# Weights summed over head groups ahead, a three-operation turn, joint normalisation of two softmaxes, and operands padded to 128 rows

## The chip, the cores and the metric

The kernel is one program on one NeuronCore of a Trainium2 chip. The metric is the device time of one execution in microseconds (us). TensorE is called PE here (its weight loads PEld), VectorE DVE, ScalarE ACT, GpSimd POOL, SyncE SP.

## The reference

Twelve layers of a decoder run one after the other over a residual of 16 batches x 128 positions x 256: four times an attention, a cross attention and a feed-forward part. The layers that the change touches are four attentions. Cut to what matters:

```
L1 attention (l1a):   q = rope(x Wq)  # 16 query heads of 16 in 4 groups
                      k = rope(x Wk), v = x Wv      # 4 heads of 16
                      # a group's queries act as one: only their sum over the group matters
                      out = softmax(causal(sum_g q . k) / 4) v Wo
L1 cross (l1x):       16 heads of 128 over 128 context rows, with a mask of context rows
L2 attention (l2a):   16 query heads, 4 key heads of 16, rms norm, rope, gain, causal softmax
L2 cross (l2x):       16 heads of 16, layer norm of q and k (affine w, b);
                      softmax over context rows 0..111 and another over rows 112..127,
                      each with its own value product; the two results are added
```

## The kernel before

Each layer is a block of its own with its own semaphores; a barrier stands between two layers, so what one layer saves the next cannot use in any other way than by starting earlier. The names of tiles begin with the layer: `l1a_`, `l1x_`, `l2a_`, `l2x_`.

**Small attentions** (`small_attention_layer`, line 3230: kind "summed" is l1a, "grouped" l2a, "split" l2x, "axial" l0x). All engines walk the same list of steps `STEPS`, and within a step each engine has a fixed order of parts; what is in flight are several batches at once. For batch b: DVE takes moments (`moments`), normalises (`normalise`), and splits into two float16 halves (`lower_norm`, line 3695); PE turns the result (`turn_norm`, line 3409), ACT copies it (`keep_norm`), PE projects (`project`, line 3421, six matmuls over halves and the two 128-row pieces of the width); DVE adds the bias (line 3720 or 3754, 3798 to 3806) and prepares q and k: for l1a in `summed_turned` (lines 3725 to 3743), which sums 256 query columns over groups to 64, copies 64 key columns, multiplies four times by cos or sin, and adds or subtracts four times. ACT and POOL then split q and k in halves (`upper_q`, `lower_q`, line 4140; `upper_k`, `lower_k`, line 4146).

Scores are made twice. `scores` (line 3494) has queries in rows; DVE reduces them to a maximum (`find_max`, line 3841), which `keep_max` (3848) writes as one more column, number KS = 48, behind the halves of q in tile `zq`. PE turns `zq` again (`turn_again`, 3507), ACT keeps it as `q2T`, and `scores_by_key` (3524 in l2a, 3535 elsewhere) computes scores with keys in rows and the maximum already subtracted: its operands have KX = 49 rows. In l2a the left operand is a slice of 49 rows of `kT`; `diagonal`, a tile into which SP's DMA spreads 48 rows of `kT` per row slot (line 3394), serves `scores` alone. ACT takes the exponential (3981), PE multiplies with the values (`heads_out`, 3553), DVE divides (`keep_out`, 3858 and 3864; in l2x twice for the two softmaxes, and 3870 adds them), ACT and POOL split the result (4037, 4151), PE turns and projects it (`turn_out` 3564, `project_out` 3572), and DVE adds it to the residual (3877).

In l1a a step is one batch, and `keep_busy` puts 11 matmuls of 256 columns without use (line 3441) into each step from that on which makes the scores of the second batch. In l2a and l2x a batch takes two steps.

**Context attention** (`context_attention_layer`, kind "merged" is l1x). Four chunks per batch, 64 in all. In each, PE adds the mask to the scores' bank by one matmul of one row (`one_row`, `mrow_b`, line 2763: 1 row x 128 columns against 1 row x 512), ahead of the 12 score matmuls (2771) and behind the 24 of the projection (2802). `mrow_b` is filled by DVE once a batch (line 2977).

## Time and profile before

| | |
|---|---|
| median of 3 runs | 3204.16 us (3202.68 to 3210.98) |
| the profiled execution | 3199.97 us |
| its span in the trace | 3198.2 us |
| PE, PEld, DVE, ACT, POOL busy | 88%, 67%, 71%, 59%, 54% |

| stage | from to, us | long, us | PE busy | DVE busy | ACT busy | POOL busy | clock granted |
|---|---|---|---|---|---|---|---|
| l1a | 588 to 737 | 149 | 120.0 | 98.2 | 68.7 | 37.1 | 0.83 |
| l1x | 737 to 1082 | 345 | 331.2 | 255.4 | 221.1 | 172.0 | 0.98 |
| l2a | 1283 to 1500 | 217 | 196.0 | 161.9 | 120.9 | 113.4 | 0.97 |
| l2x | 1500 to 1758 | 258 | 183.5 | 194.4 | 173.2 | 176.8 | 0.91 |

How to read it: an average over a stage does not tell what bounds it. The end time that the trace gives a matmul is modelled; the distance between the starts of two rows on PE is what the first one took of the engine. An engine in these stages can be busy 85% and still be the one that all others wait for, since the drains between its dependent operations are not counted as busy. The granted clock is the share of TensorE's full 2.4 GHz: 0.50 is the level of 1.2 GHz.

### The profile page before, as it was taken

Reading aid. Unit: us, or ns where it says so; the run is one execution under the profiler, and the core shown is the slowest. Engines: PE = TensorE matmul, PEld = TensorE weight load, DVE = VectorE, ACT = ScalarE, POOL = GpSimd, SP = SyncE. Lnnn points to the kernel's source line nnn. Section 1 sums busy time; section 2 is a strip of 40 time slices with the busy share of each in tenths; the row PEclk is TensorE's granted clock in tenths of the full one; section 3 lists DMA queues with packets and bytes.
Section 4 is the critical chain, followed back from the end, with each engine's and each line's share of the span. In section 5 each row is a group of like instructions: output and inputs, shape, how many; then the busy total and the mean of one; then the engine's idle time right before and its main releaser. Section 6 shows DMA issues by size and latency. Waiting matters only on the chain. (4 is left out here: it accounts for less than half of the span.)

```text
span 3198.2 us, 72026 instructions
## 1 busy us (share of the span) xinstructions
PE 2829.3 (88%) x25704; PEld 2153.0 (67%) x25739; DVE 2268.1 (71%) x5486; ACT 1887.5 (59%) x3629; POOL 1714.2 (54%) x1824
## 2 busy tenths in 40 slices
PE   7969989798999885797687899899999799998998
PEld 5757775456888654575466555688888677776665
DVE  5567764665777641786786777677777688888787
ACT  3346763355666422464676565566666588886675
POOL 2122211223555456563874366688888589887800
PEclk9999999799999886899899899999999999999999
DMA  4010001000000345000000632000000000001000
GB/s 164 1 23 14 14 9 67 7 2 8 10 7 5 121 112 117 10 6 24 13 16 14 252 89 73 3 1 0 0 0 0 6 8 6 5 5 41 29 1 27
DMA packets 95168, 104.64 MB, mean 33 GB/s; under 512 B 40716, under 2 KB 82125, under 8 KB 91984
## 3 DMA queue, kind: packets, MB, share of 16 engines
q1 hardware_dynamic: 90328, 96.08, 9.7%
q0 software_dynamic: 4608, 5.57, 1.1%
q8 instruction: 134, 2.20, 0.3%
q14 instruction: 98, 0.80, 0.1%
HBM read 80.84 MB, written 13.71 MB: 30 GB/s over the span
## 5 line engine op out<-in xcount | busy, mean ns | idle before, releaser
L2232 PE MATMUL bank<-l3a_ln_xnT,far 128*128 128x128 f16 x3072 | 194.4, 220 | 1.8 <-POOL l3a_ln_xnT L2046 1.8
L2232 PEld LDWEIGHTS bank<-l3a_ln_xnT,far 128*128 128x128 f16 x3072 | 181.7, 99 | 3.3 <-POOL l3a_ln_xnT L2046 2.2
L877 PE MATMUL bank<-l2f_xnT,l2f_wi 128*128 128x512 f16 x672 | 156.5, 381 | 7.0 <-POOLq L741 6.4
L3553 PE MATMUL bank<-l0x_v,l0x_pT 128*128 128x128 f32 x1024 | 133.9, 279 | 4.1 <-ACT l0x_pT L3981 2.5
L3553 PEld LDWEIGHTS bank<-l0x_v,l0x_pT 128*128 128x128 f32 x1024 | 126.8, 191 | 14.9 <-issue 5.8
L1226 PE MATMUL bank<-l3f_xnT,near 128*128 128x512 f16 x480 | 120.6, 388 | 6.9 <-DVE l3f_xnT L1011 3.5
L3146 POOL TENSOR_TENSOR l1x_prob<-l1x_prob,l1x_srec 128x512 f32<-128x512 f32 x64 | 66.7, 1043 | 111.1 <-DVE l1x_srec L2911 111.1
L1241 PE MATMUL bank<-near,l3f_h 128*128 128x256 f16 x960 | 119.1, 274 | 5.1 <-DVE l3f_h L1016 2.2
L877 PEld LDWEIGHTS bank<-l2f_xnT,l2f_wi 128*128 128x128 f16 x672 | 65.3, 98 | 77.8 <-POOLq L741 9.9
L1241 PEld LDWEIGHTS bank<-near,l3f_h 128*128 128x128 f16 x960 | 93.9, 98 | 34.4 <-DVE l3f_h L1016 4.1
L3841 DVE TENSOR_REDUCE l0x_smax<-bank 128x4 f32<-128x512 f32 x128 | 86.3, 686 | 29.1 <-PE bank L3494 27.0
L1025 DVE SCALAR_TENSOR_TENSOR x_res<-bank,l3f_combine,x_res 128x256 f32<-128x256 f32 x256 | 105.6, 476 | 0.1
L3981 ACT ACTIVATE l0x_pT<-bank 128x512 f32<-128x512 f32 x128 | 73.0, 596 | 52.6 <-PE bank L3535 52.6
L705 DVE TENSOR_TENSOR l2f_h<-l2f_h 128x512 f16<-128x512 f32 x56 | 59.8, 1069 | 57.6 <-ACT l2f_h L817 57.6
L2802 PE MATMUL bank<-l1x_ln_xnT,far 128*128 128x128 f16 x1536 | 96.3, 219 | 3.3 <-DVE far L2897 1.4
L2802 PE MATMUL bank<-l3x_ln_xnT,near 128*128 128x128 f16 x1536 | 96.3, 219 | 2.6 <-DVE near L2897 1.4
L3054 ACT ACTIVATE l3x_prob<-bank,l3x_less,l3x_q_rr 128x128 f32<-128x128 f32 x256 | 96.7, 461 | 1.8 <-DVE l3x_less L2934 1.3
L2154 PE MATMUL bank<-far,l3a_oT 128*128 128x256 f16 x768 | 94.3, 273 | 1.4 <-DVE l3a_oT L2339 1.4
L2825 PE MATMUL bank<-far,l1x_oT 128*128 128x256 f16 x768 | 94.3, 273 | 0.4 <-DVE x_res L2968 0.3
L2825 PE MATMUL bank<-near,l3x_oT 128*128 128x256 f16 x768 | 94.3, 273 | 0.1
L3172 POOL TENSOR_TENSOR l1x_qT<-l1x_q,l1x_qT 128x512 f16<-128x512 f32 x64 | 74.1, 1158 | 37.0 <-ACT l1x_qT L3088 36.8
L2802 PEld LDWEIGHTS bank<-l3x_ln_xnT,near 128*128 128x128 f16 x1536 | 91.1, 98 | 4.0 <-DVE near L2897 1.8
(740 smaller groups left out, 9402.0 us busy)
## 6 DMA issues: line engine op xcount, KB each, us to landing
far<-in_l1f_in SPq DMA_DIRECT2D x32, 256.0 KB, 4.4
l2f_front<-l2f_shares SPq DMA_DIRECT2D x5, 1024.0 KB
sums<-near SPq DMA_DIRECT2D x2, 2176.0 KB, 19.3
far<-in_l1f_down SPq DMA_DIRECT2D x32, 128.0 KB, 5.0
far<-sums SPq DMA_DIRECT2D x8, 512.0 KB, 7.3
l2f_wi<-in_l2f_in SPq DMA_DIRECT2D x14, 256.0 KB, 5.9
far<-l0x_kT SPq DMA_DIRECT2D x64, 48.0 KB
far<-l2x_kT SPq DMA_DIRECT2D x32, 96.0 KB
```

Of the source, the lines that this page charges most:

```text
L877: last = nc.tensor.matmul(bank[:, :], wi16[n % 2][p][:, a, k, :], xnT[q][:, k, 512 * g:512 * g + 512], start=(k + p + q == 0), stop=(k == ...
L1025: last = nc.vector.scalar_tensor_tensor(core.x[:, b, :], bank_y(k, t), weight, core.x[:, b, :], ALU.mult, ALU.add)
L1226: last = nc.tensor.matmul(b_h[f % 2][:, :], wi16[p][:, n, k, :], xnT[q][:, k, 512 * g:512 * g + 512], start=(k + p + q == 0), stop=(k == K ...
L1241: last = nc.tensor.matmul(bank_y(k, t), h16[f % LAG][q][:, P * t:P * t + P], wd16[p][:, n, :], start=(begins and p + q == 0 and t % 2 == 0 ...
L2154: last = nc.tensor.matmul(b_y[:, 0:D], oT[c % 2][q][:, P * j:P * j + P], wo(HC * c + j, 0, D, p), start=(c + j + p + q == 0), stop=(c == N ...
L2232: last = nc.tensor.matmul(bank[:, P * j:P * j + P], w(k, 512 * c + P * j, P, p), norm.xnT[u][q][:, k, :], start=(k + p + q == 0), stop=(k ...
L2802: last = nc.tensor.matmul(b_q[:, P * j:P * j + P], wq(k, 512 * c_ + P * j, P, p), norm.xnT[u][q][:, k, :], start=(k + p + q == 0), stop=(k ...
L2825: last = nc.tensor.matmul(b_y[:, 0:D], oT[c_ % 2][q][:, P * j:P * j + P], wo(HC * c_ + j, 0, D, p), start=(c_ + j + p + q == 0), stop=(c_ ...
L3054: last = nc.scalar.activation(prob[c_ % 2][:, at], b_s[:, at], ACT.Exp, bias=less[c_ % 2][:, j:j + 1], scale=q_rr[c_ % 2][:, j:j + 1])
L3172: nc.gpsimd.tensor_tensor(qT[c_ % 2][1][:, :], q32[:, :], qT[c_ % 2][0][:, :], ALU.subtract).then_inc(q_lo, 1)
L3553: last = nc.tensor.matmul(b_o[:, at:at + P], pT[f % 3][:, j, :], v_all[b % NV][:, hv:hv + P], start=True, stop=True)
L3841: last = nc.vector.tensor_reduce(smax[g % 2][:, a, 4 * u:4 * u + 4], s[:, :, lo:hi], AX.X, ALU.max)
```

## The change

- **l1a.** At the layer's start DVE sums the query weights over each group of heads (`sum_groups`, 256 columns to 64, for both 128-row pieces) into a tile of 192 columns with the key and value columns beside them, and the bias in the same way. The projection, its bias addition and its buffers have 192 columns in place of 384. The turn becomes two multiplications of 128x128, even columns by (cos, sin) and odd columns by (-sin, cos), and one addition of 128x128 that writes q and k into one tile `tok`. One semaphore, `q_ready`, tells of both.
- **l2x.** The affine bias is added to q and k in one operation of 512 columns in place of two of 256. `keep_out` takes one reciprocal of 16 columns and one multiplication of 256 in place of two of 8 and two of 128.
- **l2a.** `scores_by_key` takes its left operand from `diagonal`, all 128 rows, against all 128 rows of `q2T`. For this the DMA spreads 49 rows in place of 48 and waits for `st_made` in place of `s_made`; and POOL clears column 48 of `zq` (a memset of 128x16) in each `lower_q`, since `scores` would otherwise read a maximum left from an earlier batch.
- **l1x.** `one_row` and `mrow_b` have 128 rows, of which 127 are zero; three memsets at the layer's start are added.

```diff
-            one_row = sb("one_row", [1, P], BF16)
-            mrow_b = [sb(f"mrow_b{u}", [1, HC, P], BF16) for u in range(2)]
+            one_row = sb("one_row", [P, P], BF16)
+            mrow_b = [sb(f"mrow_b{u}", [P, HC, P], BF16) for u in range(2)]
...
-                    nc.vector.memset(one_row[:, :], 1.0)
+                    nc.vector.memset(one_row[:, :], 0.0)
+                    for u in range(2):
+                        nc.vector.memset(mrow_b[u][:, :, :], 0.0)
+                    dve.drain()
+                    nc.vector.memset(one_row[0:1, :], 1.0)
...
-    QW = 384 if causal else D
+    QW = {"summed": 192, "grouped": 384}.get(kind, D)
...
-                        after(sp, s_made, UB * R * (b - 1))
+                        after(sp, st_made if kind == "grouped" else s_made, UB * R * (b - 1))
                         for r in range(UB):
-                            rows = slice(SLOT * r, SLOT * r + KS)
+                            rows = slice(SLOT * r, SLOT * r + (KX if kind == "grouped" else KS))
...
                     if kind == "grouped":
-                        rows = slice(SLOT * u, SLOT * u + KX)
-                        last = nc.tensor.matmul(bank[:, :], kT[b % NK][rows, g % R, :],
-                                                q2T[g % 2][rows, :, :].rearrange("p j q -> p (j q)"),
+                        last = nc.tensor.matmul(bank[:, :], diagonal[b % 2][:, g % R, u, :],
+                                                q2T[g % 2][:, :, :].rearrange("p j q -> p (j q)"),
                                                 start=False, stop=True)
...
+                    if kind == "summed":
+                        for k in range(KD):
+                            sum_groups(wide_w["q"][:, k, :], weights["q"][:, k, :])
...
+                def sum_groups(to, w):
+                    nc.vector.tensor_reduce(to[:, 0:64].rearrange("p (h d) -> p h d", h=4),
+                                            w[:, 0:D].rearrange("p (h g d) -> p h d g", h=4, g=4), AX.X, ALU.add)
+                    nc.vector.tensor_copy(to[:, 64:], w[:, D:])
...
-                    nc.vector.tensor_reduce(pair[:, 0, :, :], raws[b % 2][:, 0:D].rearrange("p (h g d) -> p h d g", h=4, g=4),
-                                            AX.X, ALU.add)
-                    nc.vector.tensor_copy(pair[:, 1, :, :], raws[b % 2][:, D:D + 64].rearrange("p (h d) -> p h d", h=4))
...
+                    for a, n in enumerate(("cos", "sin")):
+                        turn = consts[n][:, :].rearrange("p (c d) -> p c d", c=2).unsqueeze(1).to_broadcast([P, 8, 2, 8])
+                        nc.vector.tensor_tensor(parts_[a], x[:, :, a, :].unsqueeze(2).to_broadcast([P, 8, 2, 8]), turn,
+                                                ALU.mult)
...
+                    nc.vector.tensor_tensor(tok[b % 2][:, :, :].rearrange("p h d -> p (h d)"), rot[:, 0:P], rot[:, P:2 * P],
+                                            ALU.add).then_inc(q_ready, 1)
...
-                        nc.vector.tensor_tensor(tok[:, :, :], four(raws[b % 2][:, :])[:, i, :, :], sb_[:, i, :, :], ALU.add
-                                                ).then_inc(ready, 1)
+                    nc.vector.tensor_tensor(tok[b % 2][:, :, :].rearrange("p (a h) d -> p a h d", a=2),
+                                            four(raws[b % 2][:, :]), sb_, ALU.add).then_inc(q_ready, 1)
...
-                    for a in range(parts):
-                        nc.vector.reciprocal(orec[:, a, 0:n], o[:, :, (HD + 1) * (a + 1) - 1])
+                    nc.vector.reciprocal(orec[:, 0:n, :], o[:, :, :, HD])
...
+                        nc.vector.tensor_tensor(o_two[:, 0:n, :, :], o[:, :, :, 0:HD],
+                                                orec[:, 0:n, :].unsqueeze(3).to_broadcast([P, n, parts, HD]), ALU.mult
+                                                ).then_inc(o_read, 1)
...
+                    if kind == "grouped":
+                        nc.gpsimd.memset(z[:, :, KS:KX], 0.0)
```

DVE in l1a, from the bias addition of one batch (`l1a_raw`) to the next residual, before:

```order
L3720 SCALAR_TENSOR_TENSOR l1a_raw<-bank,l1a_t_bias 128x384
L3681 BN_STATS l1a_stats<-x_res 128x6
L3683 BN_AGGR l1a_mv<-l1a_stats 128x2
L3685 TENSOR_SCALAR l1a_var<-l1a_mv 128x1
L3848 TENSOR_SCALAR l1a_zq<-l1a_smax 128x4
L3725 TENSOR_REDUCE l1a_pair<-l1a_raw 128x64
L3727 COPY l1a_pair<-l1a_raw 128x64
L3733 TENSOR_TENSOR l1a_rot<-l1a_pair,l1a_t_cos 128x64
L3734 TENSOR_TENSOR l1a_rot<-l1a_pair,l1a_t_sin 128x64
L3735 TENSOR_TENSOR l1a_rot<-l1a_pair,l1a_t_sin 128x64
L3736 TENSOR_TENSOR l1a_rot<-l1a_pair,l1a_t_cos 128x64
L3742 TENSOR_TENSOR l1a_q_tok<-l1a_rot 128x4x8
```

and now:

```order
L3735 SCALAR_TENSOR_TENSOR l1a_raw<-bank,l1a_bias 128x192
L3696 BN_STATS l1a_stats<-x_res 128x6
L3698 BN_AGGR l1a_mv<-l1a_stats 128x2
L3700 TENSOR_SCALAR l1a_var<-l1a_mv 128x1
L3853 TENSOR_SCALAR l1a_zq<-l1a_smax 128x4
L3744 TENSOR_TENSOR l1a_rot<-l1a_raw,l1a_t_cos 128x128
L3744 TENSOR_TENSOR l1a_rot<-l1a_raw,l1a_t_sin 128x128
L3749 TENSOR_TENSOR l1a_tok<-l1a_rot 128x128
L3883 SCALAR_TENSOR_TENSOR x_res<-bank,x_res 128x256
```

The reduction and the copy are gone, ten operations of the turn (with the three more additions that follow the last row above) have become three.

POOL in l2a, where a batch's q is split (`l2a_zq`), before:

```order
L4111 TENSOR_TENSOR l2a_rstd<-l2a_var,minus_half 128x1
L4140 TENSOR_TENSOR l2a_zq<-l2a_q_tok,l2a_zq 128x16x16
L4151 TENSOR_TENSOR l2a_o<-l2a_o_tok,l2a_o 128x256
L4116 TENSOR_TENSOR x_res<-x_res,l2a_t_out_bias 128x256
L4146 TENSOR_TENSOR l2a_zk<-l2a_k_tok,l2a_zk 128x4x16
```

and now:

```order
L4117 TENSOR_TENSOR l2a_rstd<-l2a_var,minus_half 128x1
L4147 MEMSET l2a_zq 128x16
L4148 TENSOR_TENSOR l2a_zq<-l2a_tok,l2a_zq 128x16x16
L4159 TENSOR_TENSOR l2a_o<-l2a_o_tok,l2a_o 128x256
L4122 TENSOR_TENSOR x_res<-x_res,l2a_t_out_bias 128x256
```

One memset stands ahead of the split of q; nothing else has moved there. On PE no matmul changes its place in any of the four layers: operands and widths alone differ.

DVE in l2x, from the second reciprocals of a batch to the maximum behind q and k, before:

```order
L3858 RECIPROCAL l2x_orec<-bank 128x8 x2
L3864 TENSOR_TENSOR l2x_o_two<-bank,l2x_orec 128x128 x2
L3870 TENSOR_TENSOR l2x_o_tok<-l2x_o_two 128x128
L3826 TENSOR_TENSOR l2x_raw<-l2x_raw,l2x_rr 128x512
L3831 TENSOR_TENSOR l2x_q_tok<-l2x_raw,l2x_t_affine_b 128x256
L3831 TENSOR_TENSOR l2x_k_tok<-l2x_raw,l2x_t_affine_b 128x256
L3841 TENSOR_REDUCE l2x_smax<-bank 128x4 x2
```

and now:

```order
L3862 RECIPROCAL l2x_orec<-bank 128x16
L3868 TENSOR_TENSOR l2x_o_two<-bank,l2x_orec 128x256
L3872 TENSOR_TENSOR l2x_o_tok<-l2x_o_two 128x128
L3832 TENSOR_TENSOR l2x_raw<-l2x_raw,l2x_rr 128x512
L3836 TENSOR_TENSOR l2x_tok<-l2x_raw,l2x_t_affine_b 128x512
L3846 TENSOR_REDUCE l2x_smax<-bank 128x4 x2
```

Three pairs have become one operation each; the order is the same.

## Rows read from the trace of the kernel before

**Rows 1.** Stretch, length, busy PE, PEld, DVE, ACT, POOL; clock, DMA share, GB/s.
```profile
600.00:620.00 20.00, 13.22 (x56) 6.03 (x57) 16.60 (x62) 6.17 (x18) 6.42 (x13) 0.50 0.00 2
850.00:900.00 50.00, 50.00 (x580) 41.13 (x578) 38.81 (x79) 33.86 (x66) 28.20 (x33) 1.00 0.03 8
```

**Rows 2.** Timeline of PE in l1a at full clock: start us, us, idle before.
```profile
655.32 1.15 PE L3421 MATMUL bank<-l1a_w_q,l1a_xnT 128*128 128x384 f16 x6
...
661.12 0.27 PE L3564 MATMUL bank<-ident,l1a_o 128*64 128x128 f16 x2 [0.26 <-ACT l1a_xnT L3947]
...
662.75 1.15 PE L3421 MATMUL bank<-l1a_w_q,l1a_xnT 128*128 128x384 f16 x6
```

**Rows 3.** The same in l1a's first steps.
```profile
596.85 0.61 PE L3409 MATMUL bank<-ident,l1a_xn 128*128 128x128 f16 x4 [0.19 <-DVE l1a_xn L3695]
600.02 2.08 PE L3421 MATMUL bank<-l1a_w_q,l1a_xnT 128*128 128x384 f16 x6 [2.57 <-DVE l1a_raw L3720]
603.92 0.61 PE L3409 MATMUL bank<-ident,l1a_xn 128*128 128x128 f16 x4 [1.82 <-DVE l1a_xn L3695]
...
629.89 0.61 PE L3409 MATMUL bank<-ident,l1a_xn 128*128 128x128 f16 x4
```

**Rows 4.** Timeline of DVE in l1a's first steps.
```profile
598.61 0.80 DVE L3690 TENSOR_SCALAR l1a_xn<-x_res,l1a_mv,l1a_rstd 128x256 f32<-128x256 f32 x1 [1.82 <-POOL l1a_rstd L4111]
...
600.79 0.58 DVE L3725 TENSOR_REDUCE l1a_pair<-l1a_raw 128x64 f32<-128x256 f32 x1
...
603.44 0.43 DVE L3695 TENSOR_TENSOR l1a_xn<-l1a_xn 128x256 f16<-128x256 f32 x1
```

**Rows 5.** Timeline of PE in l1x.
```profile
901.53 1.50 PE L2802 MATMUL bank<-l1x_ln_xnT,far 128*128 128x128 f16 x24
902.87 0.39 PE L2025 MATMUL bank<-ident,l1x_ln_xn 128*128 128x128 f32 x2
...
906.58 1.50 PE L2802 MATMUL bank<-l1x_ln_xnT,far 128*128 128x128 f16 x24
908.01 0.38 PE L2763 MATMUL bank<-l1x_mrow_b,l1x_one_row 1*128 1x512 bf16 x1
908.33 0.84 PE L2771 MATMUL bank<-l1x_cT,l1x_qT 128*128 128x128 f16 x12
```

**Rows 6.** Timeline of PE in l2a's last steps.
```profile
1448.69 0.38 PE L3484 MATMUL bank<-l2a_mask_b,l2a_ident_b 128*128 128x512 bf16 x1
1448.90 0.82 PE L3494 MATMUL bank<-far,l2a_qT 128*128 128x256 f16 x4
1449.56 0.38 PE L3520 MATMUL bank<-l2a_maskT_b,l2a_ident_b 128*128 128x512 bf16 x1
1449.87 0.39 PE L3524 MATMUL bank<-l2a_q2T,l2a_kT 49*128 49x512 f16 x1
1450.19 0.39 PE L3520 MATMUL bank<-l2a_maskT_b,l2a_ident_b 128*128 128x512 bf16 x1
```

**Rows 7.** Timeline of DVE in l2a, steady.
```profile
1384.63 0.26 DVE L3858 RECIPROCAL l2a_orec<-bank 128x16 f32<-128x16 f32 x1 [0.63 <-PE bank L3553]
...
1393.37 0.41 DVE L3695 TENSOR_TENSOR l2a_xn<-l2a_xn 128x256 f16<-128x256 f32 x1
```

**Rows 8.** Timeline of PE in l2a, steady.
```profile
1382.36 0.40 PE L3409 MATMUL bank<-ident,l2a_xn 128*128 128x128 f16 x4 [0.15 <-DVE l2a_xn L3695]
```

**Rows 9.** Line 3770 by itself: durations as min/median/max in ns, starts.
```profile
L3770 DVE TENSOR_TENSOR l2a_rot<-l2a_raw,l2a_t_sin x32: 312/795/847, 1294.6 to 1460.0; 128x160 f32<-128x160 f32 x32
```

**Rows 10.** Timeline of POOL in l2a, steady.
```profile
1390.13 0.88 POOL L4151 TENSOR_TENSOR l2a_o<-l2a_o_tok,l2a_o 128x256 f16<-128x256 f32 x1 [4.54 <-ACT l2a_o L4037]
```

**Rows 11.** Timeline of POOL in l2x, steady.
```profile
1625.87 5.45 POOL L4134 TENSOR_TENSOR l2x_rr<-l2x_ss,minus_half 128x32 f32<-128x32 f32 x1
```

**Rows 12.** Timeline of DVE in l2x, steady.
```profile
1631.35 0.69 DVE L3826 TENSOR_TENSOR l2x_raw<-l2x_raw,l2x_rr 128x512 f32<-128x512 f32 x1
1632.18 0.44 DVE L3831 TENSOR_TENSOR l2x_q_tok<-l2x_raw,l2x_t_affine_b 128x256 f32<-128x256 f32 x1
```

More of the change, by code:

```diff
@@ L3342, in small_attention_layer @@
             whole, angles_ready = sb("whole", [P, NB, HD], I32), sem("angles_ready")
-        q_tok = [sb(f"q_tok{u}", [P, H, HD]) for u in range(2)]
-        k_tok = [sb(f"k_tok{u}", [P, HK, HD]) for u in range(2)]
+        tok = [sb(f"tok{u}", [P, H + HK, HD]) for u in range(2)]
+        q_tok, k_tok = [t[:, 0:H, :] for t in tok], [t[:, H:, :] for t in tok]
         if kind == "summed":
-            rot, pair = sb("rot", [P, D]), sb("pair", [P, 2, 4, 16])
+            rot = sb("rot", [P, D])
         if kind == "grouped":
@@ L3351, in small_attention_layer @@
         if kind != "axial":
-            raws = [sb(f"raw{u}", [P, 512 if split else 384]) for u in range(2)]
+            raws = [sb(f"raw{u}", [P, 512 if split else QW]) for u in range(2)]
         if kind in ("grouped", "split"):
@@ L3700, in axial @@
                                                    (q_made, q_read, q_ready, zq_ready))
[L3701 removed]
+                    src, to = (b_kv[:, 0:D], k_tok[b % 2]) if second else (b_q[:, 0:D], q_tok[b % 2])
                     dve.wait_ge(made, b + 1)
@@ L3712, in axial @@
                     dve.drain()
-                    nc.vector.tensor_tensor(tok[:, :, :], tok[:, :, :], r, ALU.add).then_inc(ready, 1)
+                    nc.vector.tensor_tensor(to[:, :, :], to[:, :, :], r, ALU.add).then_inc(ready, 1)
                 def summed(b, stage):
@@ L3739, in summed_turned @@
                     after(dve, zq_ready, b - 1)
-                    for i, (tok, ready) in enumerate(((q_tok[b % 2], q_ready), (k_tok[b % 2], k_ready))):
-                        s = slice(4 * i, 4 * i + 4)
-                        nc.vector.tensor_tensor(tok[:, :, 0:8], turns_[0][:, s, :], turns_[1][:, s, :], ALU.subtract)
-                        nc.vector.tensor_tensor(tok[:, :, 8:16], turns_[2][:, s, :], turns_[3][:, s, :], ALU.add)
-                        dve.drain().then_inc(ready, 1)
+                    nc.vector.tensor_tensor(tok[b % 2][:, :, :].rearrange("p h d -> p (h d)"), rot[:, 0:P], rot[:, P:2 * P],
+                                            ALU.add).then_inc(q_ready, 1)
                 def grouped(b, stage):
@@ L3862, in keep_out @@
                     out = o_tok[:, first:first + n, :]
-                    for a in range(parts):
-                        last = nc.vector.tensor_tensor(o_two[:, a, 0:n, :] if split else out,
-                                                       o[:, :, (HD + 1) * a:(HD + 1) * a + HD],
-                                                       orec[:, a, 0:n].unsqueeze(2).to_broadcast([P, n, HD]), ALU.mult)
-                    last.then_inc(o_read, 1)
                     if split:
+                        nc.vector.tensor_tensor(o_two[:, 0:n, :, :], o[:, :, :, 0:HD],
+                                                orec[:, 0:n, :].unsqueeze(3).to_broadcast([P, n, parts, HD]), ALU.mult
+                                                ).then_inc(o_read, 1)
                         dve.drain()
-                        nc.vector.tensor_tensor(out, o_two[:, 0, 0:n, :], o_two[:, 1, 0:n, :], ALU.add)
+                        nc.vector.tensor_tensor(out, o_two[:, 0:n, 0, :], o_two[:, 0:n, 1, :], ALU.add)
+                    else:
+                        nc.vector.tensor_tensor(out, o[:, :, 0, 0:HD],
+                                                orec[:, 0:n, 0].unsqueeze(2).to_broadcast([P, n, HD]), ALU.mult
+                                                ).then_inc(o_read, 1)
                     if first + n == H:
```

36 lines of the change are left out of this document (16 added, 20 removed).

## Prediction

> **What bounds the kernel now.** I read the stage table first, then the busy time by stretches, then in each touched layer the timeline of PE, and of DVE and POOL where PE waits for them. Busy shares mislead here: l1a and l2a show PE at 81% and 90% of the stage, and only the waits printed on its rows tell which engine sets the pace.
>
> - l1a at the full clock: PE. The projection (L3421) starts at 655.32 and 662.75, a step of 7.43 us, and what PE waits for in between is ACT, a quarter of a us before `turn_out` [rows 2]. DVE is named by no wait there.
> - l1a in its first steps: the clock is 0.50 and PE is busy 13.2 of 20 us, DVE 16.6 [rows 1]. PE waits 1.82 us for DVE's `lower_norm` [rows 3]. In front of that operation DVE turns a batch, from the reduction at 600.79 to 603.44, 2.65 us [rows 4].
> - l1x: PE alone, 50.00 of 50.00 us at clock 1.00 [rows 1].
> - l2a: PE and DVE close the step together. DVE waits 0.63 us for `heads_out`, then works from 1384.63 to `lower_norm`'s end at 1393.78, 9.15 us in which no row shows a wait [rows 7], and PE waits 0.15 for a `lower_norm` before it turns the next batch [rows 8]. PE's own work beside those 9.15 us has slack.
> - l2x: the loop goes through DVE (`keep_out`, then affine, then the maximum), ACT, POOL and back to PE.
>
> **l1a.** Of the turn, the reduction, a copy, four products and four sums become two products and a sum. The chain of 2.65 us [rows 4] becomes three operations of 128 columns with a drain between the second and third; a 256-column operation costs 0.43 there [rows 4], so I take about 1.1 us for all, plus 0.2 off the narrower bias addition: 1.75 us less. The projection streams 6 x 192 = 1152 columns less, 0.96 us at 1.2 GHz and 0.48 at 2.4.
>
> First steps: from the turn at 596.85 to that at 629.89 lie five intervals, 33.04 us [rows 3]. In the first two the wait for DVE closes the loop, and each can give up to 1.75; the wait of 1.82 in the first covers it, that of the second is 1.05, and its PE part shrinks too. The other three have no wait in front of `turn_norm`: they give the projection's 0.96, a little more where ACT and DVE are also in the loop; I take 1.2, 1.0 and 1.5. Sum 7.2. The next interval, in which the clock rises, gives 0.8.
>
> Full clock: nine further steps, bound by PE [rows 2], 9 x 0.48 = 4.3. The sums of weights at the start add three reductions and three copies on DVE, up to 3 x (0.58 + 0.43) = 3.0 by rows 4, less what narrower casts save; DVE stands idle 1.82 there for POOL's `rstd` [rows 4], and the first projection waits for later things, so I take 0 and keep +1.2 (3.0 - 1.8) as the end. l1a: 7.2 + 0.8 + 4.3 = **-12.3**, from -16 (each of the first five intervals gives 1.75) to -9 (the three middle ones 0.5 each, the start +1.2).
>
> **l1x.** The trace has one-row matmuls between 128-row ones. 24 projections take 902.87 - 901.53 = 1.34 us when a 128-row operation follows, and 908.01 - 906.58 = 1.43 when the one-row mask does: 0.09 to go in. The mask takes 908.33 - 908.01 = 0.32 [rows 5]; a full-height matmul of 512 columns takes 1448.90 - 1448.69 = 0.21 [rows 6]: 0.10 to come out, beyond rounding. With all rows padded both should go, 0.19 a chunk. 62 of the 64 chunks lie in stretches like 850 to 900 where PE never idles: 62 x 0.19 = 11.8. That the gap belongs to the change of height, not to this mask, l2a supports: its 49-row matmul costs the same on both sides, 0.31 and 0.32 against 0.21 [rows 6]. Three memsets at the start, two of 512 columns, stand ahead of DVE's first copy for PE: three times 0.2, +0.7 with the drain. l1x: **-11.1**, from +0.7 (no gap closes) to -13.
>
> The Trainium skill, page "TensorEngine Tiling (Array Packing)", section "Key Properties", says that changing the tiling mode drains TensorE. The 0.10 us on either side in rows 5 and 6 agree with it.
>
> **l2a.** Two 49-row matmuls per step, with two gaps of 0.10 each, would give 0.41 a step, twice a batch; if PE alone set the pace, 32 x 0.41 = 13.1. But in the steady steps the loop closes through DVE's 9.15 us [rows 7, 8]: PE finishes its scores sooner and waits more for `lower_norm`. So nothing there. In the last eight steps, which follow rows 6, no batch is normalised or prepared any more and the chain is PE, ACT, PE: four of them give 0.41, four 0.15, since ACT's exponential stands between. 2.3 us.
>
> Against this: line 3770 on DVE takes 0.31 at its shortest and 0.80 at its median [rows 9], while POOL runs an operation with two inputs. A shift of POOL's row 4151 against DVE moves such delays about. In 1390.13's step POOL splits the output for 0.88 us after 4.54 us of idleness [rows 10]; it starts when ACT has copied what PE's shorter step releases about 0.4 earlier, and then covers another DVE operation. I take +0.1 a batch over some 13 batches, +1.3, from -0.2 to +0.5 (the 0.49 between minimum and median, once a batch): -3 to +6.5. POOL's memset of 16 columns falls into the idle 4.54; its cover gone it would cost some 0.1 to 0.2 a batch. SP's DMA now waits for `st_made`, which PE passes before it turns the next k, so nobody behind it on SP's queue waits more. The 49th row adds a fiftieth to each DMA. l2a: **-1**, from -6 to +5.
>
> **l2x.** DVE's affine pair takes 0.44 each, 0.88; one operation of 512 columns is like L3826, 0.69 [rows 12]. That is 0.2, and with the start of the second one saved I estimate 0.3 (0.2 to 0.4) less on the way to the maximum, 14 steady batches: -4. The joint division takes off DVE some 0.4, but L3826 starts at 1631.35, just as POOL's `rr` ends (1625.87 + 5.45 = 1631.32) [rows 11, 12]: DVE reaches it earlier and waits. Nothing. l2x: **-4**, from 0 (another wait closes the loop instead) to -6 (14 x 0.4).
>
> Sum: -12.3 - 11.1 - 1 - 4 = -28.4. The profiled execution took 3199.97, so its counterpart is 3171.6. The median of the three runs before lies 4.2 above the profiled one, the fastest 2.7; I add 2.7 and say **3174 us**. All four terms at their ends would give 3202.7 - 41 = 3162 (-16 - 13 - 6 - 6) and 3202.7 - 3.3 = 3199 (-9 + 0.7 + 5 + 0); they won't all fall on one side.
>
> **Rivals.**
>
> *The padding gives nothing.* The gap at a one-row matmul could belong to its operands (a new bank, bfloat16 beside float16) and stay: L3484 is bfloat16 ahead of float16 and shows 0.21 [rows 6], which speaks against it. l1x then +0.7, l2a's tail 0: -12.3 + 0.7 + 1.3 - 4 = -14.3, 3188. The Trainium skill, page "TensorE: Matmul & The Clock Gate", section "Step-by-step: what each phase is for", says that the row count doesn't matter for a weight load; by that rule alone padding buys nothing. Rows 5 and 6 show a difference beside 1 and 49 rows, which the rule doesn't cover.
>
> *POOL and DVE take l2a's and l2x's gains back.* The shift costs 0.5 a batch, +7.5 in 15 batches of l2a, and l2x's merged operation falls beside a POOL operation and gains nothing: -12.3 - 11.1 + 5.2 + 0 = -18.2, 3184. For it: the spread of rows 9; against: the shift has no reason to fall on the bad side every time. The Trainium skill, page "SBUF — State Buffer", section "🔬 SBUF: two separate sides", calls the port pair of the two an exclusive lock, which the first to start gets. The 0.31 against 0.80 of rows 9 agrees.
>
> *PE sets l2a's pace after all.* The waits of 0.63 and 0.15 [rows 7, 8] would then be slack on both sides, and 13.1 come off in place of 1: 3162. The unbroken 9.15 us speak against it.
>
> *Slower: the clock stays low in l1a.* While the clock stands at 0.50, PE is busy two thirds of the time [rows 1], and it rose only after steps in which it waited no more. With a third to a half less projection in each step PE could sit at 1.2 GHz to the layer's end. The projection takes 2.08 us at one level and 1.15 at the other [rows 2, 3], 1.8 times; a step of 7.43, all PE, would take up to 6 more at that ratio, and since part of it is not columns I take 4. Thirteen such steps: +53 on -28, so 3225; it decides from about seven steps on. Against it: `keep_busy` stays in each step, the waits for DVE shrink with the work, and what is left fills PE as before.
>
> **How the numbers follow.** The forecast has 0.64 (3164 to 3183 in itself), no gain from padding 0.12, the give-back on POOL 0.13, PE in l2a 0.07, the clock 0.04. To hold 8 in 10 the range takes in the forecast with its ends, the 3188 and the 3184, and most of the 3162: **3160 to 3190**. A measurement of this kernel tells 0.3% from no change, 9.6 us: faster means under 3194.5. Only the clock, and the bad ends of several terms at once, lie above: faster 0.93, same 0.04, slower 0.03.
>
> **What the profile after would show.** l1a: `turn_norm` in the first steps some 5.3 us apart in place of 7.07 (603.92 - 596.85), at the full clock the projection every 6.95 us. l1x: the mask matmul followed after 0.21 us and the stage 11 us shorter, PE still without idle time. l2a: 0.21 at the second matmul of `scores_by_key`, a longer wait of PE for `lower_norm`, about 1 us in place of 0.15, and the same step. l2x: `rr` waited for by DVE, the step some 0.3 shorter per batch. Wrong it would be by a clock of 0.50 in l1a past 640 us, by 0.3 at the padded mask, or by a median of the line that was 3770 that has moved.

## The result, and the profile after

| | before | after |
|---|---|---|
| median | 3207.48 us (3202.68 to 3210.98, 4 runs) | 3180.65 us (3178.75 to 3184.30, 4 runs) |
| ratio | | 0.9919 (95% interval 0.9900 to 0.9937) |
| span of the profiled execution | 3198.2 us | 3178.5 us |

The changed kernel is faster by 26 us, with 32 and 20 as the ends of the interval. The forecast was 3174, the range 3160 to 3190. The change itself was put at -28.4 us, inside those ends. The 3174 stands on the fastest run of the kernel before, 3202.68, and the median beside the changed kernel is 3207.48. Between the two profiled executions lie 19.7 us. Where they went, by the first operation of each layer on DVE (us):

| stage | before | after | difference | forecast |
|---|---|---|---|---|
| l1a | 151.11 | 140.95 | -10.2 | -12.3 |
| l1x | 342.59 | 333.83 | -8.8 | -11.1 |
| l2a | 217.15 | 214.80 | -2.3 | -1 |
| l2x | 258.43 | 256.01 | -2.4 | -4 |
| the four | | | -23.7 | -28.4 |
| all others | | | +4.0 | 0 |

The +4.0 are the cross attention of layer 0 with its feed-forward part (+2.7), the feed-forward part of layer 2 (+2.5) and that of layer 1 (-1.1). The feed-forward parts do the same work as before, and the kernels below show how far such stages wander: the cross attention of layer 0 took 303.1 to 308.6 us, the feed-forward part of layer 1 194.1 to 202.4, that of layer 2 265.0 to 268.2. The four changed stages wander too. In the profiles that left their code as it was, l1a took 148.1 to 151.2 us, l1x 341.6 to 344.8, l2a 216.5 to 218.8 and l2x 258.2 to 261.7. So a single profile tells a stage no better than to some us, which for l2a and l2x is as much as their difference in the table. That is why the readings below go by the distance of rows inside a layer.

**l1a.** PE's turns at 1.2 GHz, then two projections at the full clock (timeline of PE after: start, us, line, operation; idle before it in brackets), to set against [rows 2, 3]:

```profile
596.74 0.61 PE L3415 MATMUL bank<-ident,l1a_xn 128*128 128x128 f16 x4 [7.57 <-DVE l1a_xn L3710]
...
601.07 0.61 PE L3415 MATMUL bank<-ident,l1a_xn 128*128 128x128 f16 x4 [1.84 <-DVE l1a_xn L3710]
...
605.90 0.61 PE L3415 MATMUL bank<-ident,l1a_xn 128*128 128x128 f16 x4 [1.42 <-DVE l1a_xn L3710]
...
658.16 0.67 PE L3427 MATMUL bank<-l1a_w_q,l1a_xnT 128*128 128x192 f16 x6
...
665.12 0.67 PE L3427 MATMUL bank<-l1a_w_q,l1a_xnT 128*128 128x192 f16 x6
```

DVE's turn of a batch, to set against [rows 4]:

```profile
604.13 0.32 DVE L3744 TENSOR_TENSOR l1a_rot<-l1a_raw,l1a_t_cos 128x128 f32<-128x128 f32 x1
604.38 0.28 DVE L3744 TENSOR_TENSOR l1a_rot<-l1a_raw,l1a_t_sin 128x128 f32<-128x128 f32 x1
604.73 0.78 DVE L3749 TENSOR_TENSOR l1a_tok<-l1a_rot 128x128 f32<-128x128 f32 x1
605.43 0.41 DVE L3710 TENSOR_TENSOR l1a_xn<-l1a_xn 128x256 f16<-128x256 f32 x1
```

From 604.13 to `lower_norm` at 605.43 it is 1.30 us where it was 2.65. The addition took 0.78 in this batch, where POOL's bias addition (604.64 to 605.36) ran beside it; the median of the 16 is 0.31. The projection streams in 0.67 and starts every 6.96 us, where it was 7.43.

**l1x.** PE after, to set against [rows 5]:

```profile
895.93 1.50 PE L2802 MATMUL bank<-l1x_ln_xnT,far 128*128 128x128 f16 x24
897.27 0.38 PE L2763 MATMUL bank<-l1x_mrow_b,l1x_one_row 128*128 128x512 bf16 x1
897.48 0.83 PE L2771 MATMUL bank<-l1x_cT,l1x_qT 128*128 128x128 f16 x12
898.15 0.81 PE L2814 MATMUL bank<-l1x_pT,l1x_c 128*128 128x512 f16 x3
```

The mask is entered 1.34 us after the projection's start and left after 0.21. Both gaps are gone. But in one chunk of four PE now waits:

```profile
895.49 0.60 PE L2740 MATMUL bank<-ident,l1x_prob 128*128 128x128 f32 x4
895.93 1.50 PE L2802 MATMUL bank<-l1x_ln_xnT,far 128*128 128x128 f16 x24
```

```profile
900.11 0.60 PE L2740 MATMUL bank<-ident,l1x_prob 128*128 128x128 f32 x4
900.77 1.51 PE L2802 MATMUL bank<-l1x_ln_xnT,far 128*128 128x128 f16 x24
```

```profile
898.84 1.16 POOL L3176 TENSOR_TENSOR l1x_qT<-l1x_q,l1x_qT 128x512 f16<-128x512 f32 x1 [0.48 <-ACT l1x_qT L3092]
899.95 0.69 POOL L2046 TENSOR_TENSOR l1x_ln_xnT<-l1x_ln_whole,l1x_ln_xnT 128x256 f16<-128x256 f32 x1
```

The turn of the probabilities (L2740) is followed by the projection after 0.44 us in the first pair, after 0.66 in the second. What the second one needed is POOL's split of the batch's normalised input (L2046), which ended at 900.64; it stood behind the split of q (L3176).

The kernel before had this already in it. POOL and PE there:

```profile
910.60 0.68 POOL L2046 TENSOR_TENSOR l1x_ln_xnT<-l1x_ln_whole,l1x_ln_xnT 128x256 f16<-128x256 f32 x1
```

```profile
911.41 1.51 PE L2802 MATMUL bank<-l1x_ln_xnT,far 128*128 128x128 f16 x24
```

The split ended at 911.28, 0.13 us ahead of the projection. That is the same 0.13 as in the changed kernel (900.64 and 900.77), where PE did wait for it. PE was never idle, and POOL had nothing to spare.

**l2a.** PE, the second matmul of `scores_by_key` and the next turn; DVE, the ends of its chain, to set against [rows 6 to 8]:

```profile
1431.59 0.38 PE L3529 MATMUL bank<-l2a_q2T,far 128*128 128x512 f16 x1
1431.80 0.38 PE L3526 MATMUL bank<-l2a_maskT_b,l2a_ident_b 128*128 128x512 bf16 x1
1432.02 0.38 PE L3529 MATMUL bank<-l2a_q2T,far 128*128 128x512 f16 x1
1432.23 0.28 PE L3463 MATMUL bank<-ident,l2a_zk 128*128 128x128 f16 x2
1433.47 0.40 PE L3415 MATMUL bank<-ident,l2a_xn 128*128 128x128 f16 x4 [0.96 <-DVE l2a_xn L3710]
```

```profile
1378.06 0.26 DVE L3862 RECIPROCAL l2a_orec<-bank 128x16 f32<-128x16 f32 x1 [0.63 <-PE bank L3558]
...
1386.85 0.41 DVE L3710 TENSOR_TENSOR l2a_xn<-l2a_xn 128x256 f16<-128x256 f32 x1
```

0.21 in place of 0.32 after the matmul, and a wait of 0.96 in place of 0.15 for `lower_norm`. DVE's chain is 9.20 us long (1378.06 to 1387.26) where it was 9.15, and the step went from 11.48 to 11.54.

**l2x.** DVE and POOL, to set against [rows 11, 12]:

```profile
1611.53 0.69 DVE L3832 TENSOR_TENSOR l2x_raw<-l2x_raw,l2x_rr 128x512 f32<-128x512 f32 x1 [0.35 <-POOL l2x_rr L4140]
1612.36 0.70 DVE L3836 TENSOR_TENSOR l2x_tok<-l2x_raw,l2x_t_affine_b 128x512 f32<-128x512 f32 x1
1612.99 0.74 DVE L3846 TENSOR_REDUCE l2x_smax<-bank 128x4 f32<-128x448 f32 x2
```

```profile
1605.92 5.57 POOL L4140 TENSOR_TENSOR l2x_rr<-l2x_ss,minus_half 128x32 f32<-128x32 f32 x1
```

And DVE before, the maximum behind the pair of affine additions, the first of which starts at 1632.18 in [rows 12]:

```profile
1633.10 0.74 DVE L3841 TENSOR_REDUCE l2x_smax<-bank 128x4 f32<-128x448 f32 x2
```

The affine addition takes 0.63 from start to start where the pair took 0.92. DVE waits 0.35 for `rr`, as said; but `rr` itself takes 5.57 where it took 5.45.

### The profile page after: what moved, and what is told of

It is laid out like the page before. It is cut to its first block and busy times, and to the rows that moved or that the text cites. A ratio compares the mean times of both kernels' runs of the same rounds, so it can differ in the third digit from the quotient of the medians.

```text
span 3178.5 us, 71847 instructions
## 1 busy us (share of the span) xinstructions
PE 2810.5 (88%) x25739; PEld 2163.4 (68%) x25739; DVE 2230.1 (70%) x5303; ACT 1882.8 (59%) x3629; POOL 1717.0 (54%) x1840
## 3 DMA queue, kind: packets, MB, share of 16 engines
q0 software_dynamic: 4608, 5.57, 1.1%
## 5 line engine op out<-in xcount | busy, mean ns | idle before, releaser
L2802 PEld LDWEIGHTS bank<-l1x_ln_xnT,far 128*128 128x128 f16 x1536 | 89.7, 98 | 8.7 <-issue 3.5
L3176 POOL TENSOR_TENSOR l1x_qT<-l1x_q,l1x_qT 128x512 f16<-128x512 f32 x64 | 74.2, 1159 | 39.3 <-ACT l1x_qT L3092 39.2
```

What stands on the lines that cost most here:

```text
L2802: last = nc.tensor.matmul(b_q[:, P * j:P * j + P], wq(k, 512 * c_ + P * j, P, p), norm.xnT[u][q][:, k, :], start=(k + p + q == 0), stop=(k ...
L3176: nc.gpsimd.tensor_tensor(qT[c_ % 2][1][:, :], q32[:, :], qT[c_ % 2][0][:, :], ALU.subtract).then_inc(q_lo, 1)
```

## The experiments

Each kernel ran beside the kernel before on the same chip; differences in us are the ratio's distance from 1 times 3203.

**The l1a part alone** (the sums of weights, the narrow projection and the three-operation turn of the diff ahead).

> The kernel before with the l1a part of the change alone. My account: l1a shrinks from 151.1 us to about 141 (7 us of it in the five intervals between turns at 1.2 GHz, 3.3 in the seven intervals of steady steps, against a start that is 0.5 to 1.2 later), and nothing else moves: the profiled execution near 3190, a ratio near 0.9968. Rival, that the change's gains depend on each other: l1a gives clearly less or more than 10 us by itself. Rival, that the common tile for q and k costs something in the cross attention of layer 0 (its stage was 2.4 us longer in the profile after): that stage is 2 us longer here too, since this kernel has that tile as well.

Ratio 0.9976 (0.9965 to 0.9988), -7.7 us by the ratio. The stage took 139.75 us, and the intervals between turns were those of the changed kernel to 0.01 us, but for the one in which the clock rises (7.89 against 8.39). So the l1a gain stands by itself: the stage is 11.4 us shorter, and the interval of the ratio (3.8 to 11.2 us) holds the 10 expected, though its middle is lower. The cross attention of layer 0 took 307.2 us here; it took 308.4 in a kernel without the common tile for q and k and 304.4 in one with it, so the tile isn't its cause.

**The l1x part alone.**

> The kernel before with the l1x part alone: mask and ones padded to 128 rows, three memsets. My account: each chunk gives up the two gaps of 0.10 us beside the one-row matmul, 64 x 0.2 = 12.8; 3.0 of it come back because PE then reaches the projection of each new batch 0.22 us before POOL has split its normalised input, in 14 batches; +1.0 at the start. Stage from 342.6 to about 333.8, total near -8.8, a ratio near 0.9973. Rival, that the row count plays no role and the l1x gain came from elsewhere: no change here, L2763 still followed after 0.32.

Ratio 0.9969 (0.9959 to 0.9980), -9.9 us. The stage took 335.05, the mask 0.22 and 1.34, and the same wait in one chunk of four was there. The first mask came 0.4 us later after the layer's start than in the kernel before, not the 1.0 of the changed kernel.

**The l2a part alone.**

> The kernel before with the l2a part alone: scores by key with 128 rows. My account: PE's four matmuls per batch are 0.2 us faster each, PE waits 0.96 us for DVE before each turn in place of 0.15, and the steady step stays 11.5 us; the stage goes from 217.15 to about 214.8, by its first and last steps alone. Ratio near 0.9993. Rival, PE sets the pace: about 13 us less.

Ratio 0.9988 (0.9977 to 0.9998), -3.8 us with 0.6 and 7.4 as ends. The step was 11.54, the stage 215.97. As forecast: no gain in the steady step.

**The two halves of l2x, each alone.** First the affine addition:

```
-                    for i, (tok, ready) in enumerate(((q_tok[b % 2], q_ready), (k_tok[b % 2], k_ready))):
-                        nc.vector.tensor_tensor(tok[:, :, :], four(raws[b % 2][:, :])[:, i, :, :], sb_[:, i, :, :], ALU.add
-                                                ).then_inc(ready, 1)
+                    nc.vector.tensor_tensor(tok[b % 2][:, :, :].rearrange("p (a h) d -> p a h d", a=2),
+                                            four(raws[b % 2][:, :]), sb_, ALU.add).then_inc(q_ready, 1)
```

> The kernel before with the affine additions of l2x as one operation, the division of the two softmaxes as before. My account: DVE saves 0.29 us a batch on the loop; POOL's reciprocal square root of a batch (rr) is on the loop too and was 5.57 us after in place of 5.45. If that lengthening comes from the shorter keep_out (other operations of DVE beside it), it is absent here, and the step is 13.19 - 0.29 = 12.90; if it comes from the affine part's shift, it is here, and the step is 13.02. Stage about -4 or -2.4.

Ratio 0.9986 (0.9976 to 0.9996), -4.5 us. Steps of 12.90 to 12.91 but for one of 13.24, `rr` 5.44 to 5.45: the first of the two cases. The stage took 255.42, -3.0. Then the joint division alone (`keep_out` of the diff ahead):

> The kernel before with the two divisions of the softmaxes in l2x as one, the affine additions as before. My account: the division ends earlier and DVE then waits 0.35 us for POOL's rr; the step stays at 13.19 or gets 0.12 longer if the earlier operations of DVE fall beside rr and lengthen it. Stage 0 to +2 us. Rival, that the division is on the loop: 0.4 us a batch, -6.

Ratio 1.0005 (0.9995 to 1.0016), so the total doesn't tell this kernel from the one before. The step became 13.31 to 13.32, longer by 0.12, with `rr` at 5.57, but for one batch with `rr` at 5.44 and a step of 13.18. The stage took 261.27, which says nothing: it took 261.1 to 261.7 in three kernels with l2x as before. The batch with the short `rr` and the one behind it show what goes with what. DVE and POOL, first the batch with the short `rr`:

```profile
1615.13 5.44 POOL L4135 TENSOR_TENSOR l2x_rr<-l2x_ss,minus_half 128x32 f32<-128x32 f32 x1
```

```profile
1614.58 0.42 DVE L3863 TENSOR_TENSOR l2x_o_two<-bank,l2x_orec 128x256 f32<-128x256 f32 x1
1615.47 0.29 DVE L3867 TENSOR_TENSOR l2x_o_tok<-l2x_o_two 128x128 f32<-128x128 f32 x1 [0.46 <-issue]
```

and the next:

```profile
1628.31 5.57 POOL L4135 TENSOR_TENSOR l2x_rr<-l2x_ss,minus_half 128x32 f32<-128x32 f32 x1
```

```profile
1627.77 0.42 DVE L3863 TENSOR_TENSOR l2x_o_two<-bank,l2x_orec 128x256 f32<-128x256 f32 x1
1628.28 0.29 DVE L3867 TENSOR_TENSOR l2x_o_tok<-l2x_o_two 128x128 f32<-128x128 f32 x1
```

In the kernel before, DVE and POOL at the same place:

```profile
1639.12 0.34 DVE L3870 TENSOR_TENSOR l2x_o_tok<-l2x_o_two 128x128 f32<-128x128 f32 x1
```

```profile
1639.06 5.44 POOL L4134 TENSOR_TENSOR l2x_rr<-l2x_ss,minus_half 128x32 f32<-128x32 f32 x1
```

The addition of the two softmaxes (L3867, before L3870) reads two tiles in SBUF. Where it starts 0.03 us ahead of `rr`, `rr` is 0.13 longer: so in 9 batches here and in 9 of the changed kernel. Where it starts behind `rr`, `rr` is short: at +0.06 in 10 batches of the kernel before, with the addition at 0.34 in place of 0.29, and at +0.34 in the one batch here. The joint division brought the addition forward by about 0.1, onto the wrong side. The Trainium skill, page "SBUF — State Buffer", section "🔬 SBUF: two separate sides", says that a DVE operation with two inputs in SBUF and a GpSimd operation that reads SBUF exclude each other, the first to start keeping the port for the whole instruction. That the order of the two starts decides who pays agrees with it. The "whole instruction" does not: the addition ran inside the 5.44 us of `rr`, in those 10 batches too.

**POOL's order in l1x**, in the changed kernel:

```
                             norm.rsqrt(pool, b)
+                        if ln and c_ == 2:
+                            norm.second_half(pool, b, u)
                         if proj:
                             split_q(proj)
...
-                    if merged and ln and c_ == 2:
-                        norm.second_half(pool, b, u)
```

> The changed kernel with one thing moved: in l1x POOL splits the normalised input of a batch (line 2046) ahead of the split of q and not behind it. My account: PE's wait of 0.22 us before the projection of each new batch goes away, 14 x 0.22 = 3 us, and the chunks are 4.62 apart but for the one with the extra transposes. The split of q is 0.2 later, which has 1.5 us of slack. Total about 3 us below the changed kernel. Rival, that the 0.22 is no wait for POOL but something on PE: no change.

The stage went from 333.83 to 330.18; the distances of the masks are 4.62, 4.62, 4.62, 4.85 in place of 4.62, 4.85, 4.62, 4.85. From the first mask to the last it is 288.8 us, after 292.7 and before 302.4. POOL's split now ends 1.56 us ahead of the projection in place of 0.13. So the wait was POOL's. The median was 3178.37, the ratio 0.9915 (0.9898 to 0.9931), which by itself can't be told from the changed kernel's 0.9919; the stage can.

**384 columns again in l1a**, in the changed kernel:

```
-                            last = nc.tensor.matmul(b_q[:, 0:QW], xnT16[:, i, k, :], w16["q"][j][:, k, :],
+                            to, w = b_q[:, 0:QW], w16["q"][j][:, k, :]
+                            if kind == "summed":
+                                to = b_q[:, 0:384].rearrange("p (a n) -> p a n", a=2)
+                                w = w.unsqueeze(1).to_broadcast([P, 2, QW])
+                            last = nc.tensor.matmul(to, xnT16[:, i, k, :], w,
```

> The changed kernel with the projection of l1a streaming 384 columns again (the 192 twice), all else as changed. It tells the columns from the shorter turn on DVE. My account: the steady step of l1a goes back from 6.96 to 7.44 (+3.3 in seven intervals), the intervals at 1.2 GHz grow by up to 0.96 each where PE closes the loop (three of five) and by less where DVE does; about +8 in all, so that the turn on DVE alone is worth about 2 to 3 of the 10 us. Rival, DVE was the bound in the first steps: those keep their gain of 7, and only +4 come back.

The steady step went back to 7.44, as said, but the stage only to 143.13, +2.2 in place of +8. There are two reasons. The first is that the columns cost little in the first steps. The four intervals behind the second turn, all at 1.2 GHz, were 4.83, 3.89, 5.25 and 6.21 us; the changed kernel has 4.83, 3.80, 5.10 and 5.25, the kernel before 7.08, 5.12, 5.66 and 6.22. So the columns are worth 0, 0.09, 0.15 and 0.96 there, and only the fourth shows the projection's whole 0.96. In the first of them they only fill PE's wait for DVE, which is 0.46 in front of the third turn in place of 1.42. What the change gained in the first three intervals came nearly all from the shorter work on DVE: the expectation's rival was right for them.

The second reason is the clock. In the changed kernel and in this one (stretch, length, busy PE, PEld, DVE, ACT, POOL, then the granted clock, DMA share and GB/s):

```profile
621.31:626.31 5.00, 5.00 (x28) 2.74 (x26) 3.47 (x11) 3.73 (x8) 2.16 (x5) 0.50 0.00 2
631.31:636.31 5.00, 4.79 (x40) 2.98 (x39) 3.16 (x11) 2.44 (x5) 0.55 (x1) 0.87 0.00 0
```

```profile
616.57:621.57 5.00, 4.23 (x20) 2.09 (x21) 2.50 (x7) 1.38 (x5) 0.86 (x2) 0.50 0.00 0
621.57:626.57 5.00, 4.83 (x30) 2.40 (x29) 2.98 (x11) 3.95 (x9) 2.09 (x4) 0.66 0.01 3
626.57:631.57 5.00, 4.79 (x40) 3.12 (x39) 2.88 (x11) 3.33 (x9) 1.99 (x4) 1.00 0.01 3
```

Here it rose 33 us behind the layer's start, there 41, and the seven intervals from the second turn on sum to 39.2 us in place of 40.2, with the wider projection. Whether the columns did that is open. The moment wanders by itself: with l1a's code of before it came after 46 to 47 us in seven profiles and after 38 to 39 in two, both of them 148.1 us long as a stage in place of 151.0 to 151.2. Between the ratios of this kernel (0.9941, 0.9925 to 0.9958) and the changed one lie 7 us, with intervals that overlap.

**Two products left out of l2a's turn on DVE.** The multiplications by the sine (L3770) are left out in both kernels of this pair, so the output is another one; the first is otherwise the kernel before, the second has the padded scores by key.

```
-                    for i in range(2):
-                        lo, hi = 8 * i, 8 * i + 8
-                        nc.vector.tensor_tensor(r[:, :, lo:hi], x[:, :, 8 - lo:16 - lo],
-                                                consts["sin"][:, lo:hi].unsqueeze(1).to_broadcast([P, 20, 8]),
-                                                ALU.mult)
```

> The kernel before without the two multiplications by the sine in l2a's turn on DVE (that part of the computation is left out): 1.27 us less on DVE a batch. If DVE and PE both close the loop of l2a, PE with 0.15 us of slack, the step falls only by about 0.15 to 0.3, from 11.48 to some 11.2 to 11.35, and PE becomes the bound: -2 to -5 us. It is one half of a pair with the next kernel.

> As the last one (two multiplications by the sine left out of l2a's turn), with the 128-row scores by key added. The cut alone took the step of l2a from 11.48 to 11.16 and the stage from 217.15 to 212.3. My account, that PE sets the pace once DVE's chain is 1.27 us shorter: the padding then pays what it gives PE, 4 x 0.2 us a batch, until DVE is the bound again: a step of 10.4 to 10.7, and the stage 6 to 10 us below that of the cut alone, where the same padding was worth 1 to 2 us in the full kernel. Rival, the padding's gain doesn't reach PE's loop at all: the step stays at 11.16.

| | rows by key 49 | 128 | worth of the padding |
|---|---|---|---|
| DVE's turn whole: step, stage | 11.48, 217.15 | 11.54, 214.80 | +0.06, -2.3 |
| without the two products | 11.16, 212.27 | 10.80, 205.39 | -0.36, -6.9 |

```profile
1432.36 0.40 PE L3409 MATMUL bank<-ident,l2a_xn 128*128 128x128 f16 x4 [0.22 <-DVE l2a_xn L3694]
...
1443.15 0.40 PE L3409 MATMUL bank<-ident,l2a_xn 128*128 128x128 f16 x4 [0.22 <-DVE l2a_xn L3694]
```

The step lay a little above the 10.4 to 10.7 expected, for DVE is already the last again: PE waits 0.22 for its `lower_norm`, where it was 0.15 in [rows 8]. Where l2a was left as before, its stage took 216.5 to 218.8 us in seven profiles, and 214.1 to 216.0 in the five with the padding alone, so the -2.3 is known to about 1; the -6.9, with 0.36 a step in it, is of another size. Ratios 0.9994 (0.9984 to 1.0003) and 0.9972 (0.9960 to 0.9985).

**How many rows the mask needs.** The l1x part alone, with `one_row` and `mrow_b` of 64 and of 96 rows.

> The kernel before with the mask and the ones of l1x padded to 64 rows in place of 1. If the gap of 0.10 us on either side of a matmul is the price of another height of the array's tile (32, 64 or all 128 rows), 64 rows still pay it: the mask matmul is followed after 0.32 and entered after 1.43. If it is the price of a single row only, it is gone: 0.22 and 1.34.

> The same with 96 rows. By the account of tile heights 96 rows run as 128 and pay nothing: 0.22 and 1.34. If any operand with fewer than 128 rows pays, 0.32 and 1.43 as with 64 or 1.

```profile
900.23 1.50 PE L2802 MATMUL bank<-l1x_ln_xnT,far 128*128 128x128 f16 x24
901.67 0.39 PE L2763 MATMUL bank<-l1x_mrow_b,l1x_one_row 64*128 64x512 bf16 x1
901.99 0.84 PE L2771 MATMUL bank<-l1x_cT,l1x_qT 128*128 128x128 f16 x12
```

```profile
905.07 1.50 PE L2802 MATMUL bank<-l1x_ln_xnT,far 128*128 128x128 f16 x24
906.41 0.38 PE L2763 MATMUL bank<-l1x_mrow_b,l1x_one_row 96*128 96x512 bf16 x1
906.63 0.83 PE L2771 MATMUL bank<-l1x_cT,l1x_qT 128*128 128x128 f16 x12
```

64 rows pay 1.44 and 0.32, just as one row does; 96 rows take 1.34 and 0.22, just as 128 do. The steps say the same: 4.83 us from mask to mask in most chunks with 64 rows, 4.62 in every second one with 96. The stages took 344.23 and 335.27, the single execution of each kernel 3202.30 and 3192.24, against 3198.53 to 3206.90 in nine of the kernel before. That the gap belongs to the height of the tile into which the array is divided fits this, if 96 rows run at the full height; no trace shows which height an operand gets. The Trainium skill, page "TensorEngine Tiling (Array Packing)", section "Key Properties", says that a change of the tiling mode drains TensorE. A gap on both sides of the low matmul agrees with it.

**What the runs point to, together**: the changed kernel with POOL's order in l1x, with two divisions in l2x as before, and with the wide projection for the first six batches of l1a alone.

> The changed kernel with three edits that the runs so far point to. The divisions of l2x are two again: the step of l2x 12.90 in place of 13.02, POOL's rr 5.45, -1.5 us. POOL's order in l1x as in the run before: -3.6 in that stage. In l1a the first six projections stream the 192 columns twice, which holds PE busy while its clock is at 1.2 GHz: with 384 columns throughout the clock rose about 7 us sooner than in the changed kernel. The seven intervals from the second turn on, 40.2 us there and 39.2 with the wide projection, come to about 37.8: -2.4. All together -7 against the changed kernel, about 3173, ratio near 0.990. Rival: the narrow projection behind the sixth batch lets the clock fall again, and l1a is longer than 141.

Ratio 0.9885 (0.9869 to 0.9902), median 3167.57 (3166.53 to 3175.29): 11 us below the changed kernel by the ratios, where 7 were expected, and the fastest of all. l1x took 330.13 and the step of l2x was 12.90 with `rr` at 5.45, as said. But the stage of l2x was no shorter, 256.61 where the changed kernel has 256.00: two steps ahead of the steady ones took 13.84 and 14.64 in place of 13.58 and 12.39, the second with 3.4 us at the low clock in it. So the 1.5 us for the two divisions are shown in the step and not in the stage. l1a took 139.28: its clock did something that neither account had.

```profile
608.00:616.00 8.00, 4.94 (x37) 2.80 (x37) 5.14 (x19) 4.46 (x13) 3.55 (x8) 0.89 0.00 1
618.00:620.00 2.00, 0.99 (x8) 0.66 (x9) 1.03 (x5) 2.00 (x7) 1.26 (x2) 0.99 0.03 8
626.00:630.00 4.00, 4.00 (x20) 2.98 (x21) 0.88 (x4) 1.68 (x7) 0.61 (x2) 0.50 0.01 4
630.00:634.00 4.00, 3.65 (x36) 2.39 (x35) 2.97 (x10) 1.91 (x5) 0.55 (x1) 0.97 0.00 0
```

It rose 20 us behind the start (590.17), was back at 0.50 after 30, while the last of the wide projections (619.35) was on PE, and rose for good after 40. The seven intervals sum to 39.4 us in place of 40.2; the 37.8 expected were missed, and what the filling is worth is not more than the wander of that moment.

## Why the prediction was right or wrong, point by point

- **l1a, the turn at 1.2 GHz: right in the sum, in part by luck.** The five intervals between the second and the seventh turn fell from 33.04 to 25.94, -7.1 where -7.2 was forecast. One by one they gave 2.25, 1.32, 0.56, 0.97 and 2.02, where the prediction had 1.75, 1.75, 1.2, 1.0 and 1.5. The third was to give the projection's 0.96; the wide kernel shows 0.15 of columns in it. Why the last gave so much no run tells: in the wide kernel the clock rises within it.
- **l1a, the start: wrong, the term of the sums of weights that was put at 0.** The second turn comes 1.2 us later after the layer's start (9.76 in place of 8.58). That this is the other end of the term (3.0 - 1.8) is a coincidence. The sums of the weights took 1.3 us ahead of the weights' cast, which gave back 0.4 by being narrower, and the first normalisation came 0.5 later. The sums of the bias took another 0.6 in front of the second turn's `lower_norm`. The idle time for POOL's `rstd` lies behind that `lower_norm`; it shrank from 1.82 to 1.14 and hid this second part, so that the normalisation behind it was only 0.5 late. The first interval gave the 0.7 back: that is how it could give 2.25, more than the 1.75 allowed for any. What the start cost in the end is 0.5.
- **l1a, the interval behind:** -0.3 in place of -0.8; the clock rises in it, and by itself it was 8.39, 8.11 and 7.89 in three kernels with the same l1a. **At the full clock: right per step** (7.44 to 6.96), but only eight intervals gave it, -3.8 for the forecast 9 x 0.48.
- **l1x, the two gaps: right.** 0.10 on each side, in every chunk. **The chunks that gain: wrong**, the step "62 of the 64 chunks lie in stretches where PE never idles". PE never idled before, but in 14 batches POOL's split of the new batch ended just in time, 0.13 us ahead of the projection; once PE was faster it was late by 0.22, which took a whole chunk's gain in nearly every batch, 3 us. The run with the other order gave 3.65 back. The start was +1.0 for 0.7 in the changed kernel and +0.4 with the l1x part alone; the clock, which rose 9.6 and 8.4 us behind the layer's start (8.3 before), is likely the rest.
- **l2a: right in its mechanism**, which was the largest sum at stake (13.1). PE's saving showed as its wait, 0.96 for the forecast "about 1", and the pair of cut kernels shows that DVE's chain held it back. Even the shift against POOL came as put: POOL's L4159 starts 0.34 earlier in DVE's chain, one DVE operation (L3771) takes 0.60 in place of 0.18 and the two products 1.19 in place of 1.56, in all +0.05 a batch where +0.1 was taken. The first steps gave 1.2 that the sum didn't have; with the code as before these six intervals took 57.5 to 60.0 us in seven profiles, so this is no more than their wander. The tail gave 1.5 of the forecast 2.3.
- **l2x, the affine pair: right**, 0.29 a batch for 0.3. The sum took it 14 times; some ten steps are steady. **The joint division: wrong, the step that put it at nothing.** It was hidden, but it moved the addition behind it to 0.03 us ahead of `rr`: +0.12 a batch. The rival of a give-back between POOL and DVE was put into l2a and into the affine operation; it came here.
- **The rivals.** No gain from padding: out by the runs with 64, 96 and 128 rows. PE sets the pace of l2a: out by the pair. The clock that stays low: it rose in every kernel within 48 us of the layer's start; a narrower projection may hold it back by some us, which one profile suggests and the spread of that moment leaves open.
- **The signs named for the profile after.** Most came: the first interval 4.83 (5.3 forecast), the projection every 6.96, the mask followed after 0.21, PE's wait of 0.96 in l2a, l1a's clock up at 632.6 us and so ahead of 640. Two did not: PE in l1x was to stay without a wait and waits 0.22 a batch, and l2x's step fell by 0.17 in place of 0.3. And one sign of being wrong did show: the median of the sine's products (L3770, now L3776) moved from 795 to 422 ns. It was a poor sign, since the other operation that was held up (L3771) took it back and the chain moved by 0.05 us.
- **The ends.** The -16 for l1a doesn't follow from its own reason: five intervals at 1.75 with 0.8 and 4.3 are 13.9, so the low end of all terms is 3164 and not 3162. The clock's 3225 is counted from the profiled execution; counted as the others it is 3228. Neither touches the forecast.
- **The total.** The four stages gave 4.7 us less than forecast: 2.1 in l1a (1.2 its start, of which 0.7 came back in the first of the five intervals and is counted there; 0.5 the interval behind them, 0.4 the rest), 2.3 in l1x, 1.6 in l2x, less 1.3 that l2a gave more. With the +4.0 of the other layers they are the 8.7 us by which the profiled execution (3180.31) lies above the 3171.6 put for it. By the ratios the parts alone add up to what they give together: -7.7, -9.9, -3.8, -4.5 and +1.6 are -24.3, against -26 (20 to 32).

## What to carry to other kernels

An engine that is busy without a gap doesn't show how little slack the work that feeds it has: before counting a saving on it for every step, ask in each kind of step (here the one chunk in four with a new batch) which feeder ends how long before its use. An operation that is hidden is not free to move: taken off DVE it lets the next one start earlier, and beside a long POOL operation 0.1 us decides who waits. And an operand of few rows (1, 49 and 64 were tried) between full ones costs 0.2 us, which padding takes away where TensorE sets the pace, and only there.
